# Work of the next stage moved into the end of the stage before, at two seams of a decoder layer

## Chip, cores and metric

The kernel runs on one core of a Trainium2 chip. The metric is the device time of one execution in microseconds (us), the median of several runs. A profile of one execution comes with it: busy time of TensorE (PE; PEld is its weight load, which overlaps it), VectorE (DVE), ScalarE (ACT), GpSimd (POOL) and SyncE (SP, which here only issues loads and stores), and the clock that was granted to TensorE, as a share of 2.4 GHz.

## What is computed

One decoder layer over 8 sequences of 256 tokens of width 512, in fp32, shortened from the reference:

```python
x = layernorm(x + attention(x, Wq, Wk, Wv, Wo))          # causal, 16 query heads, 4 key heads, head size 32
Q, K, V = x @ Wq.T + bq, ctx @ Wk.T + bk, ctx @ Wv.T + bv
score = einsum('bshd,bsgd->bshg', Q, K)                  # for each token: head against head, 16 x 16
x = layernorm(x + einsum('bshg,bsgd->bshd', softmax(score), V) @ Wo.T + bo)
scores = softmax(x @ gate_weight.T)                      # 64 gates; the 6 largest are kept
soft, scalar = per-expert softmax and sum of the kept ones, 8 experts of 8
out = einsum('fth,tf->th', experts(x, soft), scalar)     # silu(gate) * up, down, each with low-rank terms
out += silu(x @ sh_gate.T) * (x @ sh_up.T) @ sh_down.T   # two shared experts of 352 columns each
x = layernorm(x + out)
```

## The kernel before

Three stages run one after another, each in a block of its own: `attention`, `cross` and `experts`. A block ends for every engine when all of them have finished it; that is what is called a seam here. Every fp32 product is made of three matmuls of a high and a low part (`three`): the high part is a rounded copy made by ScalarE, the low part the difference made by VectorE ("split"). Each engine has its own list of instructions in program order and waits on semaphores (`wait_ge`).

`attention` and `cross` go over the 8 batches (`over_batches`, `over_pipeline`), the first three or one and the last written out, the others in a loop. The order within a batch is written by hand for each engine.

In the last batch of `attention` TensorE makes three of the six projections of `cross`'s batch 0 (`context(0)` to `context(2)`: keys for both halves of the tokens and values for the first), and then ends its own stage: `values`, `output`, `turn_rows` (transposes of the normalized rows, which ScalarE copies to `x2T` in `features_out`). `cross` begins with the other three projections (`project(0, 3)` to `project(0, 5)`: values for the second half, queries for both), which want `x2T` split (`x_high`, `x_low`). GpSimd makes the mask `apart_f` there from eight corner pieces and adds the biases to the turned keys and queries (`keys_biased`, `queries_biased`); the `scores` want all of these. The output weights `o_raw` are loaded when `cross` starts, behind `v_bias` and the context of batch 1.

A batch of `cross` is, for TensorE: `scores`, four projections of the next batch, `values`, the turns of the batch before, two more projections, `outputs`. VectorE does the softmax (`less_maxima`, `reciprocals`, `probs_turned`), the tiles' transposes and the splits. In the last batch (7) there is no next one to project, so `scores(7)` is followed directly by `values(7)`, which waits for the turned probabilities.

`experts` goes over two shared (`routed` is false) and eight routed experts, each over 4 blocks (`tb`) of 512 tokens. For every block three tiles of gate and up columns are made in the order `MADE = (2, 0, 1)` into the banks `pair[slot]`, passed through the sigmoid-weighted product (`sg`, `h`), split (`HH`, `HL`) and multiplied with the down weights (`down`, `finish`). For expert 0 the logits of the gate (`logits`, `logits_turned`) are made as well. At its start the block loads the gate and expert 0's weights and splits them:

```python
sp.dma_start(g_raw[:], A["gate"]).then_inc(l_gate, 16)
landing.load_first(sp)
...
for k in range(KC):
    copy(XH[:, k, :], x2T[:, k, 0:TB]).then_inc(xh_rdy, 1)
act.wait_ge(l_gate, 16)
copy(GHL[:, :, 0:E], g_raw[:]).then_inc(gate_hi, 1)
gu_split(0, 0), gu_split(0, 1), gu_split(0, 2), dw_split(0)
```

## Time and profile before

| | us |
|---|---|
| median of 3 runs (1867.97 to 1870.09) | 1869.81 |
| the profiled execution, its own time | 1873.85 |
| its span, first to last instruction | 1872.1 |
| TensorE busy | 1755.1 (94%) |
| VectorE busy | 1233.2 (66%) |
| ScalarE busy | 707.4 (38%) |
| GpSimd busy | 267.7 (14%) |

`attention` takes the first 319 us of the span, `cross` the next 281 (up to 600), `experts` the rest. Busy times of the engines overlap. The clock column is the share of full speed that TensorE was granted; it has two levels, 1.2 GHz (0.5) and 2.4 GHz (1.0), and a mean between them is a mixture over time. Times in the rows below are counted from the start of the span.

### The profile page before, as it was taken

Reading aid. Unit: us, or ns where it says so; the run is one execution under the profiler, and the core shown is the slowest. Engines: PE = TensorE matmul, PEld = TensorE weight load, DVE = VectorE, ACT = ScalarE, POOL = GpSimd, SP = SyncE. Lnnn points to the kernel's source line nnn. Section 1 sums busy time; section 2 is a strip of 40 time slices with the busy share of each in tenths; the row PEclk is TensorE's granted clock in tenths of the full one; section 3 lists DMA queues with packets and bytes.
Section 4 is the critical chain, followed back from the end, with each engine's and each line's share of the span. In section 5 each row is a group of like instructions: output and inputs, shape, how many; then the busy total and the mean of one; then the engine's idle time right before and its main releaser. Section 6 shows DMA issues by size and latency. Waiting matters only on the chain.

```text
span 1872.1 us, 37649 instructions
## 1 busy us (share of the span) xinstructions
PE 1755.1 (94%) x14528; PEld 1426.5 (76%) x14528; DVE 1233.2 (66%) x1951; ACT 707.4 (38%) x1492; POOL 267.7 (14%) x247
## 2 busy tenths in 40 slices
PE   4789987899994999999999999999999999999997
PEld 4678875788884777778777877777787777777786
DVE  3677864677765456576676675765766766756776
ACT  4555642122121424443353343433433433434331
POOL 1345544334342000000000000000000000000000
PEclk9898987999997999999999999999999999999999
DMA  4021121000001103021030030020110300300011
GB/s 155 27 64 49 62 71 51 26 12 22 11 0 50 48 1 93 20 75 51 13 92 20 11 100 10 21 89 18 57 46 20 89 21 10 100 10 19 12 51 46
DMA packets 56850, 81.49 MB, mean 44 GB/s; under 512 B 12032, under 2 KB 31360, under 8 KB 56000
## 3 DMA queue, kind: packets, MB, share of 16 engines
q1 hardware_dynamic: 56768, 80.35, 14.1%
q8 instruction: 57, 0.93, 0.2%
q14 instruction: 25, 0.20, 0.0%
HBM read 73.50 MB, written 6.82 MB: 43 GB/s over the span
## 4 chain that ended last, share of the span: by engine, by line
PE 63%; DVE 2%; issue 2%; ACT 1%; DMA 0%; POOLq 0%; POOL 0%; DVEq 0%
PE pair L1891 10%; PE pair L1892 9%; PE pair L1893 9%; PE y_ps L1891 3%; PE y_ps L1893 3%; PE y_ps L1892 3%; PE qa_ps L1891 3%; PE qa_ps L1893 3%; PE qa_ps L1892 3%; PE pair L2029 2%; PE pair L2020 2%; PE pair L2019 2%; PE pair L2028 1%; PE qd_ps L2096 1%; PE qd_ps L2097 1%
## 5 line engine op out<-in xcount | busy, mean ns | idle before, releaser
L1891 PE MATMUL pair<-XH,GUH 128*128 128x512 f32 x800 | 316.6, 396 | 0.0
L1892 PE MATMUL pair<-XL,GUH 128*128 128x512 f32 x800 | 312.7, 391 | 0.0
L1893 PE MATMUL pair<-XH,GUL 128*128 128x512 f32 x800 | 312.1, 390 | 0.0
L1891 PEld LDWEIGHTS pair<-XH,GUH 128*128 128x128 f32 x800 | 150.3, 188 | 38.8 <-issue 7.5
L1893 PEld LDWEIGHTS pair<-XH,GUL 128*128 128x128 f32 x800 | 150.3, 188 | 32.3
L1892 PEld LDWEIGHTS pair<-XL,GUH 128*128 128x128 f32 x800 | 150.4, 188 | 30.4
L1449 POOL TENSOR_TENSOR qb_raw<-qb_raw,qb_scale 128x704 f32<-128x704 f32 x8 | 13.6, 1704 | 1046.9 <-DVE G L1603 914.6
L1459 ACT ACTIVATE HH<-h 128x512 fp32r<-128x512 f32 (+1 forms) x120 | 75.8, 632 | 176.0 <-DVE h L1810 94.2
L1603 DVE TENSOR_TENSOR HL<-h,HH 128x512 fp32r<-128x512 f32 (+1 forms) x120 | 83.1, 692 | 83.8 <-ACT HH L1459 83.8
L1805 DVE TENSOR_TENSOR h<-pair,sg 128x512 f32<-128x512 f32 x80 | 55.0, 688 | 124.2 <-ACT sg L1548 124.1
L1548 ACT ACTIVATE sg<-pair 128x512 f32<-128x512 f32 x80 | 47.9, 598 | 206.5 <-PE pair L2020 183.6
L390 ACT ACTIVATE p<-scores_ps,nm 128x128 f32<-128x128 f32 (+1 forms) x256 | 103.8, 434 | 47.4 <-DVE nm L472 42.8
L1891 PE MATMUL y_ps<-DWH,HH 128*128 128x512 f32 (+1 forms) x288 | 115.4, 401 | 5.9 <-DVE xtok L1844 3.6
L316 POOL TENSOR_TENSOR p<-p,rinv 128x512 f32<-128x512 f32 x64 | 102.0, 1600 | 118.9 <-DVE rinv L478 118.8
L1892 PE MATMUL y_ps<-DWL,HH 128*128 128x512 f32 (+1 forms) x288 | 112.9, 392 | 0.0
L1893 PE MATMUL y_ps<-DWH,HL 128*128 128x512 f32 (+1 forms) x288 | 112.9, 392 | 0.0
L1807 DVE TENSOR_TENSOR h<-pair,h 64x512 f32<-64x512 f32 x40 | 27.3, 683 | 107.1 <-ACT h L1459 106.9
L1459 ACT ACTIVATE SH<-low 128x512 fp32r<-128x512 f32 x32 | 20.2, 633 | 192.0 <-DVE low L1767 191.4
L1603 DVE TENSOR_TENSOR XL<-xe,XH 128x512 fp32r<-128x512 f32 x128 | 82.7, 687 | 1.2
L472 DVE TENSOR_REDUCE nm<-scores_ps 128x4 f32<-128x512 f32 x64 | 58.3, 953 | 31.6 <-PE scores_ps L645 31.6
L486 DVE STREAM_TRANSPOSE PB<-p 128x512 f32<-128x512 f32 x64 | 61.7, 966 | 19.4 <-PE rest_ps L667 17.6
L1891 PEld LDWEIGHTS y_ps<-DWH,HH 128*128 128x128 f32 (+1 forms) x288 | 54.2, 188 | 23.5 <-DVE xtok L1844 7.5
(341 smaller groups left out, 4204.7 us busy)
## 6 DMA issues: line engine op xcount, KB each, us to landing
gu_raw<-in_gu SPq DMA_DIRECT2D x20, 512.0 KB, 3.7
wrep<-soft_f SPq DMA_DIRECT2D x64, 128.0 KB
ws<-soft_hl SPq DMA_DIRECT2D x384, 16.0 KB
dw_raw<-in_dw SPq DMA_DIRECT2D x10, 512.0 KB, 4.4
xT_raw<-in_xT SPq DMA_DIRECT2D x8, 512.0 KB, 4.1
x_raw<-in_x SPq DMA_DIRECT2D x8, 512.0 KB, 4.1
VR<-v_rows SPq DMA_DIRECT2D x32, 128.0 KB, 2.6
out<-xtok SPq DMA_DIRECT2D x4, 1024.0 KB, 4.3
```

The costliest lines, as they stand in the source:

```text
L316: nc.gpsimd.tensor_tensor(probs[:, u], probs[:, u], rinv[:, u, 4 * unit:4 * unit + 4].unsqueeze(2).to_broadcast([P, KV, keys]), ALU.mult). ...
L390: done = nc.scalar.activation(probs[:, u, kv, :], s_ps[:, kv, unit * S:unit * S + keys], ACT.Exp, bias=nm[:, u, n:n + 1], accum_out=sums[: ...
L472: nc.vector.tensor_reduce(nm[:, u, 4 * unit:4 * unit + 4], s_ps[:, :, unit * S:unit * S + keys], AX_X, ALU.max, negate=True).then_inc(max_ ...
L486: nc.vector.transpose(turned[:, g], probs[:, u].rearrange("p v (c j) -> p (v c) j", j=32)).then_inc(pb_rdy, 1)
L1459: copy = lambda out, src: nc.scalar.activation(out, src, ACT.Copy)
L1548: nc.scalar.activation(sg[:, b, :], pair[b][0][:], ACT.Silu).then_inc(silu_rdy, 1)
L1603: sub = lambda out, a, b: nc.vector.tensor_tensor(out, a, b, ALU.subtract)
L1805: nc.vector.tensor_tensor(h[:, b, :], pair[b][1][:], sg[:, b, :], ALU.mult).then_inc(h_rdy, 1)
L1891: mm(out, wh, xh, start=first, stop=False)
L1892: mm(out, wh, xl, start=False, stop=False)
L1893: return mm(out, wl, xh, start=False, stop=last)
L2019: mm(pair[b][c][:], QBH[:, cols], S2[:], start=False, stop=False)
```

## The change

At the first seam, the last batch of `attention` makes all six projections of `cross`'s batch 0: the fourth ahead of `output`, the two query ones behind it. For that the query weights and the first 256 tokens are split there already, and the two attentions share tiles (`way.QH`, `way.QL`) and banks (`first_bank`).

```diff
                 if last:
+                    weights_high(way.l_q, WQH, way.q_raw)
+                    act.wait_ge(s_done, G * B)
+                    copy(QH[:], x2T[:, :, 0:S]).then_inc(way.high, 1)
                     features_out(b - 1, 0)
                     features_out(b - 1, 1)
                     o_high(b, 0)
                     o_high(b, 1)
-                    weights_high(way.l_q, WQH, way.q_raw)
                     features_out(b, 0)
                     features_out(b, 1)
...
                     probs_turned(b, 3, 1)
+                    weights_low(2, WQH, WQL, way.q_raw)
+                    dve.wait_ge(way.high, 4)
+                    sub(QL[:], x2T[:, :, 0:S], QH[:].bitcast(F32)).then_inc(way.low, 1)
                     o_low(b, 0)
                     o_low(b, 1)
                     residual(b, 0)
                     residual(b, 1)
                     norm_out(b, 0)
                     norm_out(b, 1)
-                    weights_low(2, WQH, WQL, way.q_raw)
...
+                if n == 4:
+                    pe.wait_ge(way.low, 4)
+                if n >= 4:
+                    pe.wait_ge(r_rdy, 2 * (B - 1) + n - 3)
                 t = slice(n % 2 * P, n % 2 * P + P)
-                wh, wl = ((way.WKH, way.WKL), (way.WVH, way.WVL))[n // 2]
+                wh, wl = ((way.WKH, way.WKL), (way.WVH, way.WVL), (WQH, WQL))[n // 2]
+                xh, xl = (QH, QL) if n >= 4 else (XH, XL)
                 for k in range(KC):
-                    three(way.projections[n], XH[:, k, t], XL[:, k, t], wh[:, k, :], wl[:, k, :], k == 0, k == KC - 1)
+                    three(way.first_bank(n), xh[:, k, t], xl[:, k, t], wh[:, k, :], wl[:, k, :], k == 0, k == KC - 1)
...
                     values(b)
                     context(2)
+                    context(3)
                     output(b, 0)
                     output(b, 1)
+                    context(4)
+                    context(5)
                     turn_rows(b, 0)
                     turn_rows(b, 1)
```

The start of `cross` on the engines: ScalarE copies the mask to its four row groups, GpSimd makes only one group of it and adds the query biases earlier, VectorE no longer splits tokens of batch 0, and turns the values of batch 0 later, in the softmax of batch 0 (`values_turned(0)` behind `reciprocals`).

```diff
-            for r in range(0, P, 32):
-                for u in range(2):
-                    part = apart_f[r:r + 32, :, u, :]
-                    nc.gpsimd.affine_select(out=part, in_=part, compare_op=ALU.is_ge, fill=NEG, base=(15, -16)[u],
-                                            pattern=[[0, 8], [0, NH]], channel_multiplier=(-1, 1)[u]).then_inc(consts, 1)
-            pool.wait_ge(consts, 10)
+            for u in range(2):
+                part = apart_f[:, :, u, :]
+                nc.gpsimd.affine_select(out=part, in_=part, compare_op=ALU.is_ge, fill=NEG, base=(15, -16)[u],
+                                        pattern=[[0, 8], [0, NH]], channel_multiplier=(-1, 1)[u]).then_inc(consts, 1)
             pool.wait_ge(way.l_b, 64)
             for s in range(2):
                 keys_biased(0, s)
-            nc.gpsimd.memset(PB[:], 0.0).then_inc(consts, 1)
+            for s in range(2):
+                queries_biased(0, s)
             pool.wait_ge(way.l_b, 80)
             for s in range(2):
                 values_biased(0, s)
-            for s in range(2):
-                queries_biased(0, s)
+            nc.gpsimd.memset(PB[:], 0.0).then_inc(consts, 1)
...
+            act.sem_inc(xh_rdy, 1)
+            copy(identR[:], ident[:]).then_inc(const_r, 1)
+            act.wait_ge(consts, 4)
+            for r in range(0, P, 32):
+                done = copy(apart[r:r + 32], apart_f[:])
+            done.then_inc(const_r, 1)
             values_out(0, 0)
-            act.wait_ge(consts, 10)
-            copy(apart[:], apart_f[:]).then_inc(const_r, 1)
-            copy(identR[:], ident[:]).then_inc(const_r, 1)
             values_out(0, 1)
...
+            dve.sem_inc(xl_rdy, 1)
             keys_turned(0, 0)
-            x_low(0)
             keys_turned(0, 1)
-            context_low(1)
             queries_turned(0, 0)
             queries_turned(0, 1)
-            values_turned(0)
-            dve.wait_ge(way.high, 4)
+            context_low(1)
+            dve.wait_ge(way.high, 5)
             sub(WOL[:], o_raw[:], WOH[:].bitcast(F32)).then_inc(way.low, 1)
             x_low(1)
...
+                if first:
+                    values_turned(0)
+                if more(b, 1):
...
+                if isinstance(b, int) and b == 0:
+                    pe.wait_ge(qt_rdy, 2)
...
-            pe.sem_inc(proj_done, 3)
-            for n in range(3, NPJ):
-                project(0, n)
+            pe.sem_inc(proj_done, NPJ)
             pe.wait_ge(const_r, 2)
```

At the second seam, expert 0's weights are loaded by SyncE at the end of its loop in `cross`, the gate when the key projections of batch 7 are done. The high and low parts of the first 512 tokens, of the gate and of the weights are made in batches 6 and 7 of `cross`, in tiles that held the attention's weights. TensorE makes the first tile and the logits between `scores(7)` and `values(7)`, and the second tile behind `outputs(7)`. The sigmoid and the product of the first tile are made in batch 7, too.

```diff
+            landing.load_first(sp)
+            sp.wait_ge(proj_done, NPJ * (B - 1) + 2)
+            sp.dma_start(ahead.g_raw, A["gate"]).then_inc(way.l_q, 16)
...
+            def experts_high():
+                copy(ahead.XH[:], x2T[:, :, 0:TB]).then_inc(ahead.high, 1)
+                act.wait_ge(landing.l_gu[NI - 1], 16)
+                copy(ahead.GUH[NI - 1][:], landing.gu[NI - 1][:]).then_inc(ahead.high, 1)
+                act.wait_ge(way.l_q, 48)
+                copy(ahead.GHL[:, :, 0:E], ahead.g_raw[:]).then_inc(ahead.high, 1)
+            def experts_high_too():
+                act.wait_ge(proj_done, NPJ * B)
+                for j in range(NI - 1):
+                    act.wait_ge(landing.l_gu[j], 16)
+                    copy(ahead.GUH[j][:, :, 0:GUW[j] // KC], landing.gu[j][:]).then_inc(ahead.high, 1)
+            def experts_silu():
+                (gate, up), sg, h = ahead.pair[0], ahead.sg, ahead.h
+                act.wait_ge(proj_done, NPJ * B + 1)
+                nc.scalar.activation(sg[0:UW, 0, :], gate[0:UW, :], ACT.Silu)
+                nc.scalar.activation(sg[LT:P, 0, :], gate[UW:LT, :], ACT.Silu)
+                copy(h[0:UW, 0, :], up[UW:2 * UW, :]).then_inc(ahead.high, 1)
+            def experts_logits():
+                act.wait_ge(proj_done, NPJ * B + 2)
+                copy(ahead.lgT[:], ahead.qa_ps[:].rearrange("p (i m) -> p i m", i=4))
...
+                if last:
+                    experts_high_too()
...
+                elif not last:
+                    experts_high()
+                if last:
+                    features_out(b - 1, 0)
+                    experts_silu()
+                    features_out(b - 1, 1)
+                    experts_logits()
...
+            def experts_x_low():
+                dve.wait_ge(ahead.high, 1)
+                sub(ahead.XL[:], x2T[:, :, 0:TB], ahead.XH[:].bitcast(F32)).then_inc(ahead.low, 1)
+            def experts_low():
+                dve.wait_ge(ahead.high, 2)
+                sub(ahead.GUL[NI - 1][:], landing.gu[NI - 1][:], ahead.GUH[NI - 1][:].bitcast(F32)).then_inc(ahead.low, 1)
+                dve.wait_ge(ahead.high, 3)
+                sub(ahead.GHL[:, :, E:2 * E], ahead.g_raw[:], ahead.GHL[:, :, 0:E].bitcast(F32)).then_inc(ahead.low, 1)
+            def experts_low_too():
+                for j in range(NI - 1):
+                    hi, lo, raw = ahead.GUH[j], ahead.GUL[j], landing.gu[j]
+                    dve.wait_ge(ahead.high, 3 + j + 1)
+                    if MADE[j] < NI - 1:
+                        done = sub(lo[:], raw[:], hi[:].bitcast(F32))
+                    else:
+                        sub(lo[:], raw[:, :, 0:P], hi[:, :, 0:P].bitcast(F32))
+                        done = sub(hi[:, :, P + UW:2 * P], raw[:, :, P:P + UW], hi[:, :, P:P + UW].bitcast(F32))
+                    done.then_inc(ahead.low, 1)
+            def experts_product():
+                (gate, up), sg, h = ahead.pair[0], ahead.sg, ahead.h
+                dve.wait_ge(ahead.high, NI + 3)
+                nc.vector.tensor_tensor(h[0:UW, 0, :], up[0:UW, :], h[0:UW, 0, :], ALU.add).then_inc(ahead.low, 1)
+                nc.vector.tensor_tensor(h[UW:LT, 0, :], gate[LT:P, :], sg[LT:P, 0, :], ALU.mult)
+                dve.wait_ge(ahead.low, NI + 3)
+                nc.vector.tensor_tensor(h[0:UW, 0, :], h[0:UW, 0, :], sg[0:UW, 0, :], ALU.mult)
...
+                if last:
+                    norm_out(b - 1, 0)
+                    norm_out(b - 1, 1)
+                    experts_low_too()
...
+                elif not last:
+                    experts_x_low()
+                else:
+                    experts_product()
...
+                elif not last:
+                    experts_low()
+                for i in range(2):
+                    residual(b, i, own, ahead.y_ps[i] if last else j_ps[i])
...
             def outputs(b, i, projected):
+                out = j_ps[i] if projected else ahead.y_ps[i]
                 if isinstance(b, int) and b == 0:
-                    pe.wait_ge(way.low, 4)
-                pe.wait_ge(ol_rdy, 2 * b + i + 1)
+                    pe.wait_ge(way.low, 5)
+                pe.wait_ge(ol_rdy, 2 * b + (i + 1 if projected else 2))
                 if projected:
                     pe.wait_ge((vr_rdy, qt_rdy)[i], 2 * (b + 1) + 2 - i)
-                else:
-                    after(pe, r_rdy, 2 * (b - 1) + i + 1)
...
+                else:
+                    turn_rows(b - 1, 0)
+                    pe.wait_ge(vr_rdy, 2 * B)
+                    pe.wait_ge(qt_rdy, 2 * B)
+                    pe.wait_ge(r_rdy, 2 * (B - 1))
+                    pe.wait_ge(ahead.low, 4)
+                    ahead.tile(0, 0, True).then_inc(proj_done, 1)
+                    turn_rows(b - 1, 1)
+                    ahead.logits().then_inc(proj_done, 1)
...
                 if last:
+                    pe.wait_ge(ahead.low, 5)
+                    ahead.tile(1, 1, True)
                     turn_rows(b, 0)
                     turn_rows(b, 1)
```

The tiles, banks and products that `cross` and `experts` share are in a new class:

```diff
+    def __init__(self, nc, ctx, way):
+        halves = lambda w: (w[:, :, 0:2 * P], w[:, :, 2 * P:4 * P])
+        self.nc = nc
+        self.XH, self.XL = way.WVH[:], way.WVL[:]
+        self.GUH = [*halves(way.WQH), halves(way.WKH)[0]]
+        self.GUL = [low if j < NI - 1 else low[:, :, 0:P] for j, low in zip(MADE, (*halves(way.WQL), halves(way.WKL)[0]))]
+        self.QAH, self.QAL = halves(way.WKH)[1][:, :, 0:P], halves(way.WKH)[1][:, :, P:2 * P]
+        self.GHL = halves(way.WKL)[1][:, :, 0:P]
+        self.g_raw = halves(way.k_raw)[1][:, :, P:P + E]
+        self.h, self.sg, self.wrep, self.ws = (t[:].rearrange("p (b k) t -> p b (k t)", b=2)
+                                               for t in (way.xh_f, way.xl_f, way.ql_f, way.QH))
...
+        bank = lambda t, n: t[:, n, :]
+        self.pair = [way.projections[0:2], [bank(way.scores, 2), bank(way.scores, 3)]]
+        self.qa_ps, self.qd_ps = way.projections[2], bank(way.rest, 0)
+        self.y_ps = [bank(way.scores, 0), bank(way.scores, 1)]
...
+    def logits(self):
+        for k in range(KC):
+            for x in (self.XH, self.XL):
+                last = self.nc.tensor.matmul(self.qa_ps[:], self.GHL[:, k, :], x[:, k, :],
+                                             start=k == 0 and x is self.XH, stop=k == KC - 1 and x is self.XL)
+        return last
+    def tile(self, b, j, closed):
+        mm, XH, XL, GUH, GUL, pair = self.nc.tensor.matmul, self.XH, self.XL, self.GUH, self.GUL, self.pair
+        def three(out, wh, wl, k):
+            mm(out, wh, XH[:, k, :], start=k == 0, stop=False)
+            mm(out, wh, XL[:, k, :], start=False, stop=False)
+            return mm(out, wl, XH[:, k, :], start=False, stop=k == KC - 1 and closed)
+        if MADE[j] < NI - 1:
...
+                    last = three(pair[b][c][:], GUH[j][:, k, cols], GUL[j][:, k, cols], k)
+            return last
```

(The rest of `tile` is the narrow tile's code, moved from `experts` as it was.) `experts` starts with signals in place of that work; the split of the down weights moves behind the first products, `selection()` to the end of the first block of tokens, and TensorE skips the two tiles that are made:

```diff
-            sp.dma_start(g_raw[:], A["gate"]).then_inc(l_gate, 16)
-            landing.load_first(sp)
             sp.dma_start(inv_i[:], A["inv"].partition_broadcast(E)).then_inc(l_inv, 16)
...
+            act.sem_inc(xh_rdy, KC)
+            act.sem_inc(gu_hi, NI)
+            act.sem_inc(lg_rdy, 1)
+            act.sem_inc(silu_rdy, 1)
...
+                        if not routed and (e, tb, j) == (0, 0, NI - 1):
+                            dw_split(0)
+                        made = not routed and (e, tb, j) == (0, 0, 0)
...
+                if (it, j) == (0, NI):
+                    selection()
...
+            dve.sem_inc(xl_rdy, KC)
+            dve.sem_inc(w_gu, NI)
+            dve.sem_inc(h_rdy, 1)
+            dve.sem_inc(tail_sum, 1)
+            nc.vector.tensor_tensor(both[:], ident[:, 0:E], ident[:, E:2 * E], ALU.add).then_inc(gate_both, 1)
...
+                        if not routed and (e, tb, j) == (0, 0, 1):
+                            dw_split(0)
...
+                    if not routed and e == 0 and tb > 0:
                         logits(tb)
                     for j, tile in enumerate(MADE):
                         b = slot(tb, j)
                         if not routed:
                             route(e, tb, j)
+                        if not routed and (e, tb) == (0, 0) and j < NI - 1:
+                            continue
...
+            pe.sem_inc(lg_done, 1)
+            pe.sem_inc(gu_done, NI - 1)
...
-        with ExitStack() as passage:
-            way = Passage(nc, passage)
-            with nc.sbuf_tensor("bo_rows", [P, D], F32) as bo:
-                attention(nc, splitter, A, ident, bo, way, v_rows, x2T, xtok)
-            cross(nc, A, ident, way, x2T, xtok)
-        landing = Landing(nc, ctx, A)
-        experts(nc, A, landing, ident, x2T, xtok, scal, soft_f, soft_hl)
+        way = Passage(nc, ctx)
+        with nc.sbuf_tensor("bo_rows", [P, D], F32) as bo:
+            attention(nc, splitter, A, ident, bo, way, v_rows, x2T, xtok)
+        landing, ahead = Landing(nc, ctx, A), Ahead(nc, ctx, way)
+        cross(nc, A, ident, way, landing, ahead, x2T, xtok)
+        experts(nc, A, landing, ahead, ident, x2T, xtok, scal, soft_f, soft_hl)
```


## Rows read from the trace of the kernel before

**Rows 1.** Windows: us, busy (count) PE, PEld, DVE, ACT, POOL; clock, DMA share, GB/s

```profile
300.00:305.40 5.40, 5.40 (x17) 4.13 (x13) 1.29 (x2) 2.88 (x3) 0.00 (x0) 0.50 0.00 2
...
311.10:320.10 9.00, 1.76 (x8) 1.13 (x8) 6.60 (x8) 2.02 (x3) 5.94 (x7) 0.75 0.00 0
...
370.00:380.00 10.00, 8.65 (x218) 7.39 (x210) 5.74 (x12) 1.26 (x2) 2.40 (x3) 0.83 0.02 5
...
593.50:604.60 11.10, 2.25 (x10) 1.49 (x9) 6.04 (x12) 3.90 (x8) 6.04 (x16) 0.59 0.27 69
...
830.00:1872.00 1042.00, 1030.49 (x4524) 819.80 (x4522) 700.35 (x1090) 398.43 (x664) 24.65 (x18) 1.00 0.14 42
```

**Rows 2.** Chain that ended last, in order of time: start us, us, what

```profile
600.04 3.49 DMA g_raw<-in_gate
...
604.57 3.75 PE qa_ps L1905 x8
...
627.98 0.50 PE y_ps L1891
```

**Rows 3.** Timeline of TensorE, first seam: start us, us, instruction, [idle before <-releaser]

```profile
333.69 2.16 PE L1116 MATMUL scores_ps<-tk,tq 32*32 32x32 f32 x136 [1.84 <-issue]
...
339.06 0.79 PE L1077 MATMUL rest_ps<-xWkH,aXH 128*128 128x512 f32 x1
...
351.96 3.54 PE L1132 MATMUL scores_ps<-pb,xVT 128*32 128x32 f32 x215
```

**Rows 4.** Timeline of VectorE, first seam

```profile
332.06 2.00 DVE L975 STREAM_TRANSPOSE xVT<-vr 128x1024 f32<-128x1024 f32 x1
333.95 2.24 DVE L950 TENSOR_TENSOR xWoL<-xWoL_raw,xWoH 128x2048 fp32r<-128x2048 f32 x1
336.12 1.21 DVE L950 TENSOR_TENSOR xXL<-x2T,xXH 128x1024 fp32r<-128x1024 f32 x1
339.20 0.69 DVE L980 TENSOR_REDUCE xtop<-scores_ps 128x16 f32<-128x512 f32 x1 [1.88 <-PE scores_ps L1116]
...
344.55 5.69 DVE L995 STREAM_TRANSPOSE pb<-pr 32x512 f32<-32x512 f32 x8
```

**Rows 5.** Timelines of ScalarE and GpSimd, first seam

```profile
329.24 1.92 ACT L883 ACTIVATE xWoH<-xWoL_raw 128x2048 fp32r<-128x2048 f32 x1 [1.39 <-DMA xWoL_raw<-in_xwo]
...
315.71 3.14 POOL L326 TENSOR_TENSOR xtok<-xs,bo_rows 128x512 f32<-128x512 f32 x1 [0.47 <-DVE xs L510]
319.18 0.10 POOL L838 MEMSET xhalf<- 128x2 f32 x1 [0.33 <-POOLq L166]
...
331.52 2.07 POOL L807 TENSOR_TENSOR tq<-tq,qk_bias 128x512 f32<-128x512 f32 x2
```

**Rows 6.** Timeline of TensorE, second seam

```profile
579.86 2.87 PE L1132 MATMUL scores_ps<-pb,xVT 128*32 128x32 f32 x171 [10.81 <-DVE pb L995]
...
587.68 0.48 PE L1077 MATMUL rest_ps<-xWoH,xOH 128*128 128x512 f32 x1
...
596.00 1.12 PE L1152 MATMUL rest_ps<-ident,xxs 128*128 128x128 f32 x4 [2.48 <-DVE xxs L1022]
...
625.01 0.40 PE L1891 MATMUL y_ps<-DWH,HH 96*128 96x512 f32 x1
```

**Rows 7.** Timelines of VectorE and ScalarE, second seam

```profile
569.09 0.69 DVE L980 TENSOR_REDUCE xtop<-scores_ps 128x16 f32<-128x512 f32 x1 [4.06 <-PE scores_ps L1116]
...
586.69 1.29 DVE L950 TENSOR_TENSOR xOL<-scores_ps,xOH 128x512 fp32r<-128x512 f32 x2 [6.06 <-ACT xOH L883]
...
612.34 1.82 DVE L1603 TENSOR_TENSOR DWL<-dw_raw,DWH 128x1024 fp32r<-128x1024 f32 x2 [1.66 <-ACT DWH L1459]
...
550.86 1.09 ACT L883 ACTIVATE xOH<-scores_ps 128x512 fp32r<-128x512 f32 x2 [3.53 <-PE scores_ps L1132]
...
610.73 1.58 ACT L1459 ACTIVATE DWH<-dw_raw 128x1024 fp32r<-128x1024 f32 x2 [1.30 <-DMA dw_raw<-in_dw]
```

**Rows 8.** The page's costliest groups: busy us, mean ns of one, idle before

```profile
L1891 PEld LDWEIGHTS pair<-XH,GUH 128*128 128x128 f32 x800 | 150.3, 188 | 38.8 <-issue 7.5
```

170 lines of the change are left out of this document (76 added, 94 removed).

## The prediction

> **What bounds the kernel now.** I read the busy time by stretch first. From 830 us to the end TensorE is busy 1030.5 of 1042 us, 4,524 matmuls at 0.230 us each, and the change leaves that work as it is; the time to be had is where TensorE waits [rows 1]. Around the first seam (first attention to second) it is busy 1.76 of 9.0 us, around the second (second attention to experts) 2.25 of 11.1 us. In both the granted clock is below 1, and in the stretch after work resumes it still is, so a wait costs twice: in itself, and in matmuls of 0.43 instead of 0.23 us. Second came the chain of work that ended last: it begins at 600.04 with the load of the gate weights and goes over their splits to the logits, which run at half clock (3.75 us for 8), and from there over TensorE [rows 2]. Ahead of 600 us the chain is cut at the block's boundary, so the engines' timelines in the two seams were the third view [rows 3 to 7]: there the reader is to see who ends each wait of TensorE.
>
> TensorE's work is the same before and after; it is moved into waits. So the gain is waiting removed and clock won, less waiting added.
>
> **Seam 1.** Moved from the second attention's start to the first one's end: one value projection (12 matmuls) ahead of the outputs, two query projections (24) behind them, the splits of the query weights and of the first tokens. The splits now run while TensorE does the last values product and VectorE and ScalarE have nothing to do but wait for it, so they cost nothing. Were they late, a split of weights and one of tokens (2.2 and 1.2 us by the like ones in [rows 4]) would stand ahead of the queries. At full clock 12 matmuls take 12 x 0.230 = 2.75 us. The clock is 0.50 up to 305.4 [rows 1] and full in the outputs behind, so the value projection takes 2.75 us and the outputs end at 313.85 instead of 311.1. The queries fill 313.85 to 319.35, mostly former wait, and hold up the turns of the normalized rows by 2 us. Two turns and the copies behind them end near 321.1. Before, the block's last work ended at 318.85: a GpSimd addition that took 3.14 us beside VectorE's weight split [rows 5] and that now runs without it. Second attention starts at 321.4 instead of 319.2: 2.2 us later, 36 projections ahead.
>
> There the first scores want the turned tiles and four bias additions (2.07 us for two [rows 5]), behind two corner masks instead of eight: 321.4 + 1.6 + 4.1 = 327.1. They take 5.4 us (333.69 to 339.06 [rows 3]) and end at 332.6, 6.5 us earlier than before. But VectorE can't use this. Its queue holds, ahead of the softmax, the splits of the output weights and of batch 1's tokens, and these wait for a 1 MB load issued when the block starts: ScalarE began its copy at 329.24, released by the DMA, 10.0 us after the start, and took 1.92 [rows 5]. After: copy 331.4 to 333.3, VectorE's split to 335.6, tokens (1.21) to 336.8. The softmax starts there instead of at 339.20. Up to the last turned probabilities (344.55 + 5.69 = 350.24) it took 11.0 us [rows 4]; the values' transpose (2.00) is moved into this stretch, where 0.25 us was wait, so 12.8: 349.6. TensorE meanwhile has 12.9 us of projections from 332.7 on (339.06 to 351.96 before), ends them near 347, since one waits for the keys' transpose, and waits. Its values product starts at 349.7 instead of 351.96: **-2.3 us**. Bounds: 0, if 2.3 us more of half clock or of queueing loads come on top; -6.3, if the output weights don't hold VectorE (332.8 + 12.8 = 345.6).
>
> **Seam 2.** In batch 6 ScalarE gets 3.4 us of copies (2048, 1024 and 256 columns) into its wait of 3.53 us ahead of the attention output [rows 7]; they just fit. One of them waits for the gate load, now issued by SyncE some 5 us before, and behind it the attention output is queued. Five raw loads of the experts, 2 MB, go out near 490 instead of 600, at the end of SyncE's queue, and nobody is behind them. VectorE's splits fall into its waits. All this costs nothing; a microsecond late would still be covered by the three projections (8 us) that TensorE has ahead of the outputs.
>
> In batch 7 TensorE waited 10.81 us for the probabilities [rows 6]. Into this go two turns (0.65 each), 20 matmuls of the first tile (4.6) and 8 of the logits (1.85): 7.75 us, some 9 with half clock at first. So 579.86 stays. All at half clock would be 14 us, 3 us too late; a bound.
>
> Behind the values the two turns are gone. The outputs now wait for both halves of the attention output's split, since they write to banks that it is read from: 586.69 + 1.29 = 587.98 [rows 7], so 588.05 instead of 587.68: +0.4, and behind this wait stand the second tile and the last turns. TensorE stands still for 2.5 us before it. In 370 to 380, where it lost 1.35 us to waiting, the mean clock was 0.83 [rows 1]: 3.4 us at half, worth 1.7. I take the same here: +1.7 (0 to 3.4). The outputs end at 595.6 instead of 593.5, the second tile (24 x 0.230 = 5.5) at 601.1. Then turns, copies and the block's end: 596.00 to 600.04 before [rows 2, 6], of which 0.8 was half clock, so 3.2: 604.3. In the experts' block the logits' turn (0.4 + 0.85) and the third tile (5.5) end at 611.05; half clock for part of it, +0.9 (0 to 1.7): 611.9. The down weights' split, now in this block, takes 1.58 on ScalarE and 1.82 on VectorE [rows 7], behind a sigmoid, a product, two copies and two splits (some 3.3 us): ready 6.7 us after the start, at 611.0, just covered by the third tile. Before, that tile ended at 625.01, and the wait up to 627.98 hangs on its own copy, product and splits [rows 2, 6], which stay. 625.0 - 611.9: **-13.1 us**, bounds -10 to -16.
>
> Of such pauses the Trainium skill (TensorE: Matmul & The Clock Gate, "Why this matters for your kernels") counts only longer ones as harmful. The stretch of 370 to 380 shows half clock after 1.35 us of waiting, so the page and the trace differ and I go by the trace; by the page the 1.7 and the 0.9 us would fall away and the sum would be -18.0.
>
> **Sum.** -2.3 - 13.1 = -15.4 us. The profiled execution took 1873.85 us with a span of 1872.1; the median of the runs is 1869.81. The span should become 1856.7 and the median **1854.4 us** (-0.82%). Two tenths of a per cent, 3.7 us, is about what a measurement of this kernel can tell from no change.
>
> **Rivals.**
> - Clock and handovers take more: seam 1 gives 0, seam 2 gives 10 (outputs, second and part of the third tile at half clock): 1860, mixtures from 1858. For it: TensorE now stands still in more and shorter pieces, and a short one in 370 to 380 was followed by half clock. Against: the long waits are gone. 0.18.
> - The output weights don't hold VectorE, seam 1 gives 6.3, total 19.4: 1850.4. For it: two of the other queued jobs are gone. Against: the same three loads in the same order. 0.10.
> - The clock is kept through the short waits: -18.0, 1851.8. For it: in 311.1 to 320.1 the clock's mean is 0.75 though TensorE stood for 7.2 of 9.0 us [rows 1], so it outlasts some waiting. Against: 370 to 380. 0.10.
> - Slower: the experts' weight tiles become halves of 512-column tiles. If that lengthens each weight load past its cover, all 4,524 matmuls after 830 us pay. A load takes 188 ns [rows 8] of a period of 230, so 42 ns are free; 3.4 ns more (4,524 x 3.4 ns = 15.4 us) eat the gain, so from 46 ns it turns, and at 50 ns the kernel takes 1890. Against: the 128 columns of one load are adjacent either way. 0.04.
> - It does nothing: the same mechanism at 45 to 46 ns, within 0.2%. The other way to it, splits that delay batch 7's softmax as long as they fill, has little room: VectorE has 4.06 us there [rows 7] for two normalizations (1.0) and splits of 2.4, and even twice as long they cost 2 to 3 us. 0.03.
>
> The forecast itself has 0.55, with its own range 1852 to 1858. The range for 8 in 10 is 1850 to 1861; it leaves out the last two rivals and the ends of the others. Faster 0.93, same 0.03, slower 0.04.
>
> **What the profile after would show.** Seam 1: matmuls without a break from 300 to 319; the second attention's first instruction near 321.4, its first scores near 327, its softmax near 336.8 right behind two splits, its values product near 349.7. Seam 2 (all 2.3 us earlier by then): matmuls between 567 and 577 behind the scores; outputs after a wait of 2.5 us; the experts' first instruction near 602.0 instead of 600.0, without a gate load; the third tile's end near 609.6. From there the same work 15.4 us earlier. It would be wrong if batch 7's values product starts later than 577.6, if TensorE waits for the down weights, or if matmuls after 830 take over 0.231 us.

## The result, and the profile after

| | before | after |
|---|---|---|
| median of runs on one chip, us | 1869.95 (1867.97 to 1873.33, 4 runs) | 1854.34 (1852.83 to 1857.67, 4 runs) |
| profiled execution, its own time, us | 1873.85 | 1857.67 |
| its span, us | 1872.1 | 1855.9 |
| TensorE busy, us | 1755.1 | 1753.7 |

The ratio of the times is 0.9914, 95% interval [0.9895, 0.9934]: 15.6 us less by the medians, 16.2 by the two spans. The two profiled executions are slower than their kernels' medians, by some 3 to 4 us each. TensorE's busy time stayed (1755.1 and 1753.7 us); its waits went.

Windows of the kernel after (us, then busy and count of PE, PEld, DVE, ACT, POOL; then clock, DMA share, GB/s), where [rows 1] shows the windows of before:

```profile
304.20:318.90 14.70, 14.70 (x70) 12.17 (x68) 5.42 (x10) 0.12 (x1) 3.90 (x4) 1.00 0.00 0
318.90:331.50 12.60, 3.58 (x141) 3.00 (x140) 3.73 (x5) 6.33 (x11) 10.92 (x11) 0.60 0.45 147
...
580.80:583.30 2.50, 0.02 (x2) 0.00 (x0) 1.29 (x2) 1.08 (x2) 0.00 (x0) 1.00 0.02 7
583.30:588.00 4.70, 4.67 (x13) 3.72 (x14) 0.03 (x1) 0.00 (x0) 0.00 (x0) 0.64 0.00 0
596.00:600.00 4.00, 1.37 (x10) 0.91 (x9) 0.22 (x1) 1.71 (x3) 0.88 (x3) 1.00 0.00 0
600.00:608.00 8.00, 8.00 (x33) 6.60 (x34) 4.23 (x6) 2.69 (x5) 3.13 (x13) 0.79 0.65 192
```

The first row is the filled end of the first attention: no wait up to 318.9. The second is what is left of seam 1: 9.0 of its 12.6 us are waits of TensorE, while transfers take 0.45 of the DMA engines' time. In seam 2 the wait of 2.5 us ahead of the outputs (third row) and the half clock behind it (fourth, 0.64) are there. In the fifth row TensorE still waits for the block to end and for the logits' turn; from 600 on it is busy without a break, though not at full clock (last, 0.79).

Timeline of TensorE after, the rows with a wait in seam 1 and then in seam 2 (start, us, instruction, [idle before <-releaser]), for [rows 3] and [rows 6]:

```profile
323.03 1.22 PE L1211 MATMUL scores_ps<-apart,xidentR 128*128 128x256 f32 x4 [3.94 <-ACT apart L906]
325.39 2.17 PE L1221 MATMUL scores_ps<-tk,tq 32*32 32x32 f32 x135 [1.14 <-issue]
331.51 1.94 PE L1221 MATMUL scores_ps<-tk,tq 32*32 32x32 f32 x121 [3.96 <-issue]
348.30 3.44 PE L1237 MATMUL scores_ps<-pb,xVT 128*32 128x32 f32 x214 [2.62 <-issue]
...
574.88 2.23 PE L1237 MATMUL scores_ps<-pb,xVT 128*32 128x32 f32 x132 [1.92 <-DVE pb L1056]
578.65 2.16 PE L1237 MATMUL scores_ps<-pb,xVT 128*32 128x32 f32 x124 [1.53 <-issue]
583.33 0.50 PE L1178 MATMUL scores_ps<-xWoH,xOH 128*128 128x512 f32 x1 [2.51 <-DVE xOL L1011]
...
599.90 1.07 PE L2083 MATMUL rest_ps<-xWkL_raw,WQL_raw 128*128 128x64 f32 x8 [1.77 <-DVE xWkL_raw L1892]
```

The wait of 10.81 us ahead of batch 7's values product is now 1.92. The third row was not foreseen: in the middle of the 256 score matmuls TensorE stands for 3.96 us, and the profile shows no engine that releases it (`issue`). The kernel before has this wait too, behind the row of 136 matmuls in [rows 3], but shorter:

```profile
337.19 1.94 PE L1116 MATMUL scores_ps<-tk,tq 32*32 32x32 f32 x120 [1.35 <-issue]
```

Timeline of VectorE after, seam 1, for [rows 4]:

```profile
328.88 1.23 DVE L1011 TENSOR_TENSOR aXL<-c_raw,aXH 128x1024 fp32r<-128x1024 f32 x1 [6.02 <-ACT aXH L906]
332.19 2.29 DVE L1011 TENSOR_TENSOR xWoL<-xWoL_raw,xWoH 128x2048 fp32r<-128x2048 f32 x1 [2.08 <-ACT xWoH L906]
334.39 1.22 DVE L1011 TENSOR_TENSOR QL<-x2T,QH 128x1024 fp32r<-128x1024 f32 x1
335.53 0.68 DVE L1041 TENSOR_REDUCE xtop<-scores_ps 128x16 f32<-128x512 f32 x1
...
342.50 5.69 DVE L1056 STREAM_TRANSPOSE pb<-pr 32x512 f32<-32x512 f32 x8
```

The softmax starts at 335.53 right behind the two splits, 2.1 us after the scores ended (331.51 + 1.94 = 333.45), with no wait of its own. The last row explains the 2.62 us ahead of the values product, which the profile marks `issue` too: the probabilities' transposes end at 348.19 (342.50 + 5.69), and TensorE starts at 348.30.

### The profile page after: what moved, and what is told of

It is laid out like the page before. It is cut to its first block, busy times and chain, and to the rows that moved or that the text cites. A ratio compares the mean times of both kernels' runs of the same rounds, so it can differ in the third digit from the quotient of the medians.

```text
span 1855.9 us, 37650 instructions
## 1 busy us (share of the span) xinstructions
PE 1753.7 (94%) x14528; PEld 1426.6 (77%) x14528; DVE 1232.7 (66%) x1948; ACT 707.1 (38%) x1492; POOL 266.0 (14%) x241
## 4 chain that ended last, share of the span: by engine, by line
PE 63%; issue 2%; DVE 2%; ACT 1%; POOLq 0%; POOL 0%; DVEq 0%
PE rest_ps L1334 5%; PE scores_ps L1334 5%; PE rest_ps L1336 5%; PE rest_ps L1335 5%; PE scores_ps L1336 5%; PE scores_ps L1335 5%; PE rest_ps L2064 4%; PE rest_ps L2065 4%; PE rest_ps L2066 4%; PE scores_ps L2064 3%; PE scores_ps L2065 3%; PE scores_ps L2066 3%; PE rest_ps L2248 1%; PE rest_ps L2249 1%; PE rest_ps L1350 1%
## 5 line engine op out<-in xcount | busy, mean ns | idle before, releaser
L1772 DVE TENSOR_TENSOR HL<-aXH_raw,HH 128x512 fp32r<-128x512 f32 (+1 forms) x120 | 83.5, 696 | 83.6 <-ACT HH L1622 83.6
L2064 PE MATMUL scores_ps<-DWH,HH 128*128 128x512 f32 (+1 forms) x288 | 115.2, 400 | 5.9 <-DVE xtok L2017 3.3
L2065 PE MATMUL scores_ps<-DWL,HH 128*128 128x512 f32 (+1 forms) x288 | 113.2, 393 | 0.0
L2066 PE MATMUL scores_ps<-DWH,HL 128*128 128x512 f32 (+1 forms) x288 | 112.9, 392 | 0.0
L1334 PE MATMUL rest_ps<-xWvH,WQH 128*128 128x512 f32 x240 | 96.0, 400 | 0.0
L1334 PE MATMUL scores_ps<-xWvH,WQH 128*128 128x512 f32 x240 | 95.4, 397 | 0.0
L1335 PE MATMUL rest_ps<-xWvL,WQH 128*128 128x512 f32 x240 | 93.9, 391 | 0.0
L1336 PE MATMUL rest_ps<-xWvH,WQL 128*128 128x512 f32 x240 | 93.9, 391 | 0.0
L1336 PE MATMUL scores_ps<-xWvH,WQL 128*128 128x512 f32 x240 | 93.6, 390 | 0.0
L1335 PE MATMUL scores_ps<-xWvL,WQH 128*128 128x512 f32 x240 | 93.5, 390 | 0.0
```

The source lines that it names most:

```text
L1334: mm(out, wh, XH[:, k, :], start=k == 0, stop=False)
L1335: mm(out, wh, XL[:, k, :], start=False, stop=False)
L1336: return mm(out, wl, XH[:, k, :], start=False, stop=k == KC - 1 and closed)
L1772: sub = lambda out, a, b: nc.vector.tensor_tensor(out, a, b, ALU.subtract)
L2064: mm(out, wh, xh, start=first, stop=False)
L2065: mm(out, wh, xl, start=False, stop=False)
```

## The experiments

The profiled executions are compared by stages between the same instructions. V is the start of the first value projection in seam 1, E the start of the experts' block; all in us.

| kernel | V to first values product | that to batch 7's scores | these to its values product | to outputs | to first turn | to E | E to first addition | that to end |
|---|---|---|---|---|---|---|---|---|
| before | 51.82 | 211.50 | 16.40 | 7.82 | 8.32 | 4.05 | 28.93 | 1243.1 |
| after | 49.06 | 210.27 | 16.31 | 8.45 | 12.71 | 3.08 | 12.76 | 1244.0 |
| after_again | 46.21 | 209.25 | 16.32 | 8.39 | 12.70 | 3.07 | 12.82 | 1243.6 |
| seam1_only | 48.01 | 209.98 | 15.98 | 7.56 | 8.32 | 3.82 | 28.24 | 1242.5 |
| seam2_only | 51.82 | 210.26 | 15.99 | 8.40 | 11.19 | 3.07 | 12.79 | 1242.3 |
| warm | 47.90 | 210.75 | 16.03 | 9.21 | 11.09 | 3.08 | 14.08 | 1243.2 |
| wo_first | 47.64 | 211.11 | 16.03 | 8.14 | 11.19 | 3.07 | 12.81 | 1242.4 |
| old_banks | 47.81 | 210.82 | 16.60 | 7.84 | 12.74 | 3.07 | 12.76 | 1243.1 |
| late_load | 56.76 | 210.74 | 15.94 | 8.68 | 12.72 | 3.08 | 12.79 | 1242.4 |
| soft_first | 47.70 | 208.70 | 15.88 | 8.49 | 12.74 | 3.07 | 12.83 | 1243.3 |
| soft_late | 44.93 | 211.18 | 16.58 | 8.45 | 12.75 | 3.08 | 12.79 | 1243.9 |
| soft_late_ob | 44.35 | 210.32 | 16.31 | 7.84 | 11.20 | 3.07 | 12.79 | 1243.5 |
| best_warm | 44.71 | 210.61 | 15.88 | 7.76 | 11.10 | 3.07 | 12.80 | 1243.1 |

Where the code is the same, the stages still differ from execution to execution: the second column by 1.0 us between after and after_again and by 1.5 between before and seam1_only, the last by up to 1.7, and the first by 2.9 between after and after_again. That is the noise in which one execution's sum is to be read.

**1. Each seam alone.** seam1_only is the kernel before with the first seam's edits; seam2_only is the changed kernel with them undone (the same edit both ways, cut to its core, here as it is undone):

```diff
                 if last:
-                    weights_high(way.l_q, WQH, way.q_raw)
-                    act.wait_ge(s_done, G * B)
-                    copy(QH[:], x2T[:, :, 0:S]).then_inc(way.high, 1)
...
-                    context(3)
                     output(b, 0)
                     output(b, 1)
-                    context(4)
-                    context(5)
...
-            pe.sem_inc(proj_done, NPJ)
+            pe.sem_inc(proj_done, 3)
+            for n in range(3, NPJ):
+                project(0, n)
```

> The kernel before with the first seam's part of the change alone; second seam as before. The theory: the second attention starts about 1 to 2 us later, its softmax of batch 0 starts right behind the splits of the output weights, and its first values product starts 2.3 to 2.8 us earlier than before, counted from the first values projection (before: 351.96 - 300.14 = 51.8 us); time 1867.4 against 1869.9. The rival, that the projections moved (22 us of work after 311 before) show in full: 6.3 us less, 1863.6.

> The changed kernel with the first seam put back as it was before; second seam as changed. The theory: the two seams don't touch each other, so this gives 12 to 13 us against before, 1857.3, with the values product of batch 7 and all behind it at the same distances as in the changed kernel (outputs 8.4 us behind the start of the values product, experts' first instruction 24.2 behind it). The rival, that the gain at the second seam depends on what the first one left: a distance that differs by over 1 us.

Measured, beside runs of the kernel before with a median of 1870.86: seam 1 alone 1866.57, ratio 0.9977 [0.9967, 0.9987]; seam 2 alone 1856.76, ratio 0.9918 [0.9899, 0.9937]. So by the medians seam 1 gives 4.3 us (2.4 to 6.2 by the interval), more than the 2.5 expected, and seam 2 14.1 (11.8 to 18.9). The stages of the table say the same: V to the first values product 3.8 less with seam 1 alone, unchanged to 0.01 with seam 2 alone. Seam 2 works without seam 1; each gain belongs to its own edit.

One distance missed what was expected of seam2_only: the experts' start came 22.7 us behind batch 7's values product (8.40 + 11.19 + 3.07), not 24.2, and 1 us was set as the sign that seam 2 depends on seam 1. The 1.5 us are half clock behind the outputs' start, which this execution did not have. wo_first and soft_late_ob, which have the first seam's change, show 11.2 there too, so it is not seam 1 that decides it (see experiment 5).

**2. Output weights first.** The order of the loads at the second attention's start, and of their copies and splits, is turned round; GpSimd clears the probabilities' array ahead of the values' bias.

```diff
-            sp.dma_start(v_bias[:], A["xbv"].partition_broadcast(P)).then_inc(way.l_b, 16)
-            context(1)
             sp.dma_start(o_raw[:], A["xwo"]).then_inc(way.l_q, 16)
+            context(1)
+            sp.dma_start(v_bias[:], A["xbv"].partition_broadcast(P)).then_inc(way.l_b, 16)
```

> The changed kernel with the load of the output weights issued first of the three when the second attention starts, and its two splits ahead of those of the context. The theory, that this load held VectorE's queue ahead of the softmax of batch 0: the weights land 3 to 4 us earlier, the softmax starts right behind the scores (2.1 us earlier against the rest) and the values product with it, until TensorE's own projections bind; 2.1 us less than the changed kernel, 1852.2. The rival, that the softmax waits for the scores in any case because TensorE stands still in them for 4 us: nothing, or the stall grows with the order of the loads.

Measured: 1851.17, ratio 0.9891 [0.9874, 0.9907]. The weights landed 5.1 us after their issue instead of 9.0, and their split was over at 328.8, ahead of the scores' end at 330.89. The softmax still started only at 333.18: the context's and the tokens' splits behind it took 2.30 and 2.29 us instead of 1.2; GpSimd's addition of the values' bias ran at the same time up to 332.17. The queue of VectorE held it again, with other work. The wait inside the scores fell to 2.11 us, which pointed to the loads.

**3. The softmax ahead of the splits.** Only VectorE's order changes:

```diff
             context_low(1)
-            dve.wait_ge(way.high, 5)
-            sub(WOL[:], o_raw[:], WOH[:].bitcast(F32)).then_inc(way.low, 1)
-            x_low(1)
...
                     keys_turned(b + 1, 1)
+                if first:
+                    x_low(1)
+                    dve.wait_ge(way.high, 5)
+                    sub(WOL[:], o_raw[:], WOH[:].bitcast(F32)).then_inc(way.low, 1)
```

> VectorE's queue in the second attention's start: the output weights' split and batch 1's tokens' split stand behind batch 0's probabilities instead of ahead of its softmax; loads and everything else as in the changed kernel. Theory of the prediction (these two hold the softmax): the softmax starts with the end of the scores (some 2.3 to 2.8 us earlier against the start of the value projection than in the changed kernel's 36.3) and the values product comes 2 to 2.8 us earlier: 1852.0. Rival: TensorE's own queue of four projections, whose second half needs the keys' transposes, or the late end of the scores sets it: then the values product moves by under 0.8 us and the time stays at 1854 to 1855.

Measured: 1852.89, ratio 0.9897 [0.9878, 0.9917]. Timeline of VectorE in this kernel:

```profile
327.83 1.23 DVE L1011 TENSOR_TENSOR aXL<-c_raw,aXH 128x1024 fp32r<-128x1024 f32 x1 [5.54 <-ACT aXH L906]
333.29 0.69 DVE L1041 TENSOR_REDUCE xtop<-scores_ps 128x16 f32<-128x512 f32 x1 [4.24 <-PE scores_ps L1222]
```

The softmax now waits for the scores and starts as they end (333.24). That it was VectorE's queue that held it is shown. But the values product came only 1.4 us earlier than in the trace after, not 2 to 2.8, since the scores themselves ended late: their wait was 4.30 us here. Counted from the first scores, which leaves out the clock behind V, it came after 21.2 us, against 21.9 to 22.9 in the five executions with the changed kernel's first seam (after, after_again, seam1_only, warm, old_banks). So the order of VectorE's queue is worth some 1 us in the stages; by the times alone, wo_first and soft_first can't be told from the changed kernel, since the intervals of their ratios overlap its interval.

**4. What is the wait inside the scores?** Two kernels take loads away from beside them. late_load holds the context's and the output weights' load until the first scores are done; soft_late is experiment 3 with the output weights' load alone held:

```diff
             context(1)
+            sp.wait_ge(s_done, 1)
             sp.dma_start(o_raw[:], A["xwo"]).then_inc(way.l_q, 16)
...
                     values_out(b + 1, 0)
+                    if first:
+                        act.wait_ge(way.l_q, 32)
+                        copy(WOH[:], o_raw[:]).then_inc(way.high, 1)
```

In late_load the new wait stands ahead of `context(1)` instead, and nothing else is edited.

> The loads of the second attention's context and output weights (1.5 MB) are held until the first scores are done; the values bias's load stays early. My theory: the waits inside the first scores, which no engine ends (1.35 us before, 3.96 after, 2.11 with the output weights' load first), come from these loads taking the way to memory from TensorE's instructions. Then the scores lose about 1.35 us or less instead of 3.96, and the whole is some 5 us slower than the changed kernel, because the context's and the weights' splits come late and VectorE's softmax with them. Rival: the waits belong to the position in the program, not to the loads: then the scores still lose 3 to 4 us.

> As the run before, and the 1 MB load of the output weights is held until the first scores are done (its copy on ScalarE moved behind the softmax's exponentials), so only the context's 0.5 MB load and the bias run beside the scores. If the loads cause the waits inside the scores, these fall from 3.96 to under 2 us, and the time falls by another 2 us, to 1850; if only the position in the program does, the scores still lose 3 to 4 us and the time equals the run before.

Measured: late_load 1865.33 in its one run, its scores' wait 1.56 us; soft_late 1851.72, ratio 0.9889 [0.9869, 0.9909], its wait 1.69. Windows from the scores' start to where they go on, first the kernel after, then soft_late (the last two columns are the DMA share and GB/s):

```profile
325.39:331.51 6.12, 2.17 (x135) 2.04 (x136) 1.23 (x1) 2.33 (x2) 5.82 (x3) 0.50 0.42 170
```

```profile
326.84:330.70 3.86, 2.17 (x136) 2.04 (x136) 1.31 (x1) 1.83 (x2) 3.86 (x3) 0.50 0.01 4
```

The matmuls before the wait are the same 2.17 us; the rest is wait. The DMA queues point to a cause. In each of the two stretches there is one packet of a queue called instruction; its rows, after from 329.00 to 329.50 and soft_late from 328.00 to 328.50 (packets, MB, share of 16 engines):

```profile
q8 instruction: 1, 0.02, 11.0%
```

```profile
q8 instruction: 1, 0.02, 10.9%
```

The packet starts at 329.18 and 328.27, and the scores go on 2.3 and 2.4 us behind it (331.51 and 330.70). It takes no more time beside the loads (11.0% and 10.9% of the same half microsecond); it comes later: 3.2 to 4.0 us after the scores' start in the six kernels with the loads beside it, 1.8 in wo_first, 0.9 to 1.4 in the six without. In all thirteen traces the break sits at the same place (behind 135 or 136 of 256 matmuls) and ends 2.3 to 2.7 us behind the start of such a packet, and its length goes with the loads beside it:

| DMA share from the scores' start to where they go on | kernels | wait, us |
|---|---|---|
| 0.01 to 0.02 | before, seam2_only, late_load, soft_late, soft_late_ob, best_warm | 1.28 to 1.69 |
| 0.32 | wo_first | 2.11 |
| 0.42 to 0.48 | after, after_again, seam1_only, old_banks, warm, soft_first | 3.48 to 4.30 |

That the loads lengthen the wait is shown; that TensorE has run out of instructions there, and that their next block is held up by 1.75 MB of data, is how I read the packet. The breaks in batch 7 support the reading: in the trace after, its scores stand for 1.32 us and its values product for 1.53, with the DMA engines all but idle, and both go on 2.6 us behind such a packet. Before the change the scores came 14 us behind the block's start and its loads and met idle DMA engines; the change moved them into the loads. Of this the Trainium skill (Runtime: NRT & Kernel Launch, "Instruction fetch mechanics") says that the crossing from one block of instructions to the next is mostly hidden; these traces differ in the first scores, with 1.28 us at best and 3.5 to 4.3 beside loads. They agree where the matmuls are large: from 611 us to the end of the kernel after there are 22 such packets and no wait of TensorE without a releaser.

late_load is 11 us slower in its one run than the median of the changed kernel, where 5 were expected; 7.7 of them stand between V and the values product (56.76 in its trace against 49.06). It shortens the wait and holds VectorE with two late splits instead. In soft_late the values product comes 2.8 us earlier than in soft_first (44.93 and 47.70), where 2 were expected; the medians differ by 1.2, which four times each can't tell from nothing. The moved load pays only once VectorE's queue is rearranged as well.

**5. The clock around the last outputs.** warm puts 22 matmuls whose result nobody reads into the wait ahead of batch 7's outputs; old_banks gives these outputs their former banks, so that each waits for its own half:

```diff
+                if last:
+                    pe.wait_ge(xt_rdy, 2 * b)
+                    for _ in range(22):
+                        mm(way.rest[:, 0, 0:256], identR[:], apart[:].rearrange("p m u h -> p (m u h)"), start=True, stop=True,
+                           skip_group_check=True)
                 outputs(b, 0, not last)
```

```diff
-                out = j_ps[i] if projected else ahead.y_ps[i]
+                out = j_ps[i]
...
-                pe.wait_ge(ol_rdy, 2 * b + (i + 1 if projected else 2))
+                pe.wait_ge(ol_rdy, 2 * b + i + 1)
+                if not projected and i == 0:
+                    pe.wait_ge(ahead.low, NI + 4)
```

> The changed kernel with 22 matmuls of 256 columns without use (into a bank that is free, 0.107 us each at full clock, 2.35 us in all) in TensorE's 2.5 us wait ahead of the last outputs of the second attention. The theory, that this wait is followed by 3.4 us at half clock and so costs 1.7 us twice over: the clock stays 1.0 through the outputs, which take 5.6 instead of 7.3 us; 1.7 us less than the changed kernel, 1852.6. The rival, that the clock falls there for another reason or that the fill delays the outputs as much: no gain, 1854.3.

> The last batch's outputs go back to the banks that they had before the change (those of the first tile of the experts, whose product is done), so each of them waits only for its own half of the attention output's split; the second tile waits for both halves. Theory: the wait ahead of the outputs gets 0.6 us shorter (2.5 to 1.9) and with it the time, 0.5 us, too little for three rounds to tell; the outputs can still meet half clock. Rival, that the 2.5 us standstill sets the clock: if 1.9 us let it stand at full, the outputs also run in 5.6 us instead of up to 7.1, and the gain is 1.5 to 2.

Measured: warm 1855.67, ratio 0.9909 [0.9883, 0.9935]; old_banks 1853.42, ratio 0.9908 [0.9888, 0.9929]. With warm the outputs ran at full clock (11.09 us to the first turn instead of 12.71), but they started 0.8 us later and the third tile met more half clock (14.08 instead of 12.76): no gain. In old_banks the wait was 1.92 instead of 2.51 us, as expected, and half clock came all the same (12.74). But 11.19 us, too, occur without a fill, behind the same wait. The two waits of seam2_only in batch 7, and its window from the outputs on:

```profile
578.26 2.21 PE L1224 MATMUL scores_ps<-pb,xVT 128*32 128x32 f32 x133 [3.36 <-DVE pb L1048]
586.66 0.50 PE L1169 MATMUL scores_ps<-xWoH,xOH 128*128 128x512 f32 x1 [2.50 <-DVE xOL L1003]
```

```profile
586.66:592.00 5.34, 5.34 (x23) 4.34 (x24) 1.73 (x4) 0.00 (x0) 0.21 (x1) 1.00 0.01 3
```

The clock is 1.00 there and was 0.64 in the trace after, so the wait's length alone doesn't decide it. The half clock fell elsewhere: here the first tile and the logits ran at full clock, so that TensorE waited 3.36 us for the probabilities instead of 1.92, and the clock was 0.51 in the values product behind (578.5 to 582.0), whose small matmuls took no longer (133 in 2.21 us; in the trace after 132 took 2.23 at full clock). wo_first shows the same (a wait of 3.36, clock 0.50 from 573.5 to 576.9). What places the half clock is not shown.

**6. All together**, beside the changed kernel again. soft_late_ob is soft_late with old_banks; best_warm adds 10 of the unused matmuls.

> The changed kernel once more, unchanged, beside the next two on one chip and with more rounds: 1854.3 within a microsecond. Its profile shows whether the outputs of the last batch meet half clock (12.7 us from their start to the first turn) or not (11.2), which differed between executions of like kernels, and whether the wait inside the first scores again ends some 2.5 us behind the one instruction packet that the trace shows there, as in all traces so far.

> The three edits that helped or did no harm together: the output weights' load behind the first scores, its split and the tokens' split behind the first probabilities, and the last outputs in their former banks. By the stages of the traces 4.1 us less up to the first values product and 0.6 less ahead of the last outputs: 1854.3 - 4.7 = 1849.6. Rival: the gains don't add, because the later load meets VectorE's transposes and the projections of batch 1: 1851.7, as without the banks.

> As the run before, and 10 matmuls of 256 columns, whose result nobody reads, in the wait ahead of the last outputs (22 of them delayed the outputs by 0.8 us before). They fill some 1.3 of 1.9 us. If the wait's length sets the half clock behind it, outputs and second tile take 11.2 us instead of 12.7 in the profile, and the median falls by up to 1.5 us to 1848.1; if not, or if the clock is then lost a little later, nothing changes: 1849.6.

Measured: the changed kernel 1854.24 (expected 1854.3; its trace has half clock behind the outputs' start, 12.70, and a wait of 3.49 us in the first scores that ends 2.3 us behind the packet), ratio to before 0.9918 [0.9896, 0.9941]; soft_late_ob 1850.50, 0.9894 [0.9871, 0.9917]; best_warm 1851.07, 0.9889 [0.9866, 0.9913]. Against the changed kernel on the same chip the means of six times differ by 4.0 us for soft_late_ob (1854.67 and 1850.64; a t interval over these times gives 1.0 to 7.1). The stages say as much: 3.1 us up to the first values product (44.4 to 44.9 in soft_late, soft_late_ob and best_warm, against 46.2 to 49.1, mean 47.8, in the five with the changed kernel's first seam) and 0.6 ahead of the last outputs. The median 1850.5 lies between the 1849.6 expected and the 1851.7 of the rival that the gains don't add, so that stays open. The unused matmuls add nothing that can be told: the clock was full behind them, but it was in soft_late_ob without them too.

## Why the prediction was right

The median came out at 1854.3, forecast 1854.4. That they agree to 0.1 us is chance: the four runs span 1852.8 to 1857.7. The sum was closer than its terms; counted from V in seam 1 and from batch 7's values product in seam 2:

| step | predicted | measured |
|---|---|---|
| V to second attention's start | 21.3 | 20.9 |
| V to first scores | 27.0 | 26.2 |
| scores' length | 5.4 | 8.1 |
| V to softmax | 36.7 | 36.3 |
| V to first values product | 49.6 | 49.1 |
| **seam 1** | **-2.3** | **-2.8** |
| batch 7's values product to outputs | 8.2 | 8.45 |
| outputs to first turn | 13.05 | 12.7 |
| first turn to E | 3.2 | 3.1 |
| E to third tile's end | 7.6 | 8.8 |
| **seam 2**, up to the third tile | **-13.1** | **-12.1** |

- **Seam 1** held by its main step: the two splits, not the scores, set the softmax. Its size was low. The 2.8 us are those of one execution with half clock behind V, as before had; the five executions with this first seam give 2.8 to 5.6 us up to the values product (mean 4.0), and the times of seam1_only 4.3 (2.4 to 6.2). The scores took 2.7 us more than [rows 3] have, by the instruction wait; this cost nothing, since VectorE's splits ended 2.1 us later still. The prediction took this length from a trace in which the loads had long landed. It is also why the rival in which the output weights don't hold VectorE (6.3 us) falls short with these loads: soft_first removes the hold and gets 4.1 from V, soft_late removes both and gets 6.9, each with half clock behind V.
- The GpSimd addition of 3.14 us at the first attention's end took 1.29 without VectorE's split beside it, and the corner masks 0.62 us for two.
- **Seam 2.** The fill left a wait of 1.92 us before batch 7's values product, and its start moved by no more than the seam ahead: batch 7's scores to values 16.31 against 16.40. Outputs +0.6 against +0.4, and half clock behind them as in the forecast (12.7 against 11.2 in executions without it: 1.5, forecast 1.7). The mis-sized term is the experts' start up to the third tile's end: 8.8 us instead of 7.6. The logits' turn began 0.8 us after E instead of 0.4, and the tile took 7.1 us where it has 5.5 at full clock, so 1.6 of half clock instead of 0.9. Timeline of TensorE after, the tile's first, ninth and tenth matmul and the first down product:

```profile
600.78 0.47 PE L1334 MATMUL rest_ps<-xWvH,xWkH 128*128 128x512 f32 x1
...
604.00 0.63 PE L1336 MATMUL rest_ps<-xWvH,xWkL 128*128 128x512 f32 x1
604.42 0.48 PE L1334 MATMUL rest_ps<-xWvH,xWkH 128*128 128x512 f32 x1
...
607.91 0.39 PE L2064 MATMUL scores_ps<-DWH,HH 96*128 96x512 f32 x1
```

  Up to 604.4 a matmul lasts 0.63 (one each 0.43), then 0.39 (one each 0.23): most of nine at half clock. In executions without half clock behind the outputs the stretch from the values product to the first addition took 35.2 to 35.5 us instead of 37.0 (seam2_only, wo_first), so seam 2 gives 12 to 14 us.
- **The down weights** were covered. Timeline of VectorE after:

```profile
604.20 1.82 DVE L1772 TENSOR_TENSOR DWL<-dw_raw,DWH 128x1024 fp32r<-128x1024 f32 x2 [0.77 <-ACT DWH L1622]
...
611.88 0.69 DVE L2017 TENSOR_TENSOR xtok<-scores_ps,xtok 128x512 f32<-128x512 f32 x1 [0.46 <-PE scores_ps L2066]
```

  The split ended at 606.02, 6.9 us after E (forecast 6.7), 1.9 ahead of the third tile's end at 607.9. From there to the first addition are 3.97 us, as before (625.01 to 628.98): what was said to stay stayed.
- **The rest.** The profiled span differs by 16.2: 0.9 ahead of V, 2.8 and 12.1 in the seams, 1.3 between, and 0.9 given back behind the first addition. These other terms are no larger than the differences between executions of the same code in the table. That seam 1's half microsecond and seam 2's one cancelled, and these with them, is luck of about 1 us; against the times of each seam alone (4.3 and 14.1) both terms, 2.3 and 13.1, were low, the first just below its interval.
- **The weight layout** did nothing. Window of the kernel after, as long as the last one in [rows 1]:

```profile
814.00:1856.00 1042.00, 1030.27 (x4520) 819.49 (x4518) 700.03 (x1090) 397.44 (x663) 24.64 (x18) 1.00 0.14 42
```

  TensorE is busy 1030.3 us for 4,520 matmuls, before 1030.5 for 4,524: one each 0.228 us in both. From the first addition to the end it is 1244.0 against 1243.1 us.
- **The Trainium skill on short pauses** (TensorE: Matmul & The Clock Gate, in the prediction): its -18.0 would need both clock terms gone. The clock after the pauses was 0.64 and 0.79 in the traces of after; in other executions of like code the first was full. The Trainium skill's rule that only longer pauses harm holds in some executions, mine from [rows 1] in the others; neither in each.

## What to carry to other kernels

Work pulled forward over a stage's boundary fills waits as far as the engines' queues let it, so price what is queued ahead of the next consumer, and then take it out: here two splits in VectorE's queue, one load in SyncE's and the former banks of the last outputs were worth another 4.0 us (1.0 to 7.1) on top of 15.6. A long run of small matmuls should not share its time with big loads: here the wait inside it grew from 1.3 to 1.7 us to 3.5 to 4.3. When a wait has no releaser, look first for a producer that ended just before it, as ahead of 348.30, and then for the queue called instruction. An edit of 1 or 2 us can't be judged by one execution; compare stages between the same instructions over several traces.

## What the runs showed of the hardware

- A wait of TensorE at a fixed place among 256 small matmuls, 1.28 to 1.69 us with idle DMA engines and 3.48 to 4.30 with loads beside it; the matmuls go on 2.3 to 2.7 us after the start of a packet of the instruction queue.
- The granted clock at one place differs between executions of the same code. Windows of the changed kernel in two executions, first the trace after, then after_again:

```profile
298.00:304.00 6.00, 6.00 (x45) 4.60 (x34) 1.29 (x2) 1.08 (x2) 0.00 (x0) 0.50 0.01 4
```

```profile
298.00:304.00 6.00, 5.71 (x56) 4.65 (x56) 1.29 (x2) 1.09 (x2) 0.00 (x0) 1.00 0.01 4
```

  Half clock for some 5 us of work behind V costs 2.3 us: the first scores start 26.15 us after V in the one and 23.83 in the other. That is as much as the whole forecast for seam 1, and it is most of the difference of 49.06 and 46.21 in the table. What decides it stays open.
- GpSimd and VectorE slow each other: GpSimd's two copies into the tokens, 1.25 us before and in seam1_only, took 3.31 after, where VectorE now splits the experts' first tokens beside them (128x2048, 2.35 us); in wo_first two splits that take 1.2 us in the trace after took 2.3, beside GpSimd's additions of the values' bias, which took 4.16 us for two instead of 2.51.
